# A graph layer on one core: one chain of sums per message, node rows loaded by SyncE, self-loop products placed between products

## The reference, cut to what matters

```
h     = relu(layernorm(x))
W_rel = einsum('rb,bdf->rdf', w_comp, weight)          # 32 types from 8 bases
agg   = segment_sum(h[src] * norm, etype * n_nodes + dst)
node  = einsum('rnd,rdf->nf', agg, W_rel) + h_bias + h @ loop_weight
out   = x + relu(node)
```

## Time and profile before

| | |
|---|---|
| median of three executions | 1019.91 us |
| the profiled execution, own time | 1018.97 us |
| its span | 1017.2 us |
| granted TensorE clock | 0.995 |
| TensorE matmul busy | 992.6 us, 98% |
| VectorE busy | 955.0 us, 94% |
| ScalarE busy | 885.2 us, 87% |
| GpSimd busy | 724.0 us, 71% |
| DMA | 154.47 MB, 152 GB/s |

### The profile page before, as it was taken

How to read it: one execution, slowest core, us unless ns; L and a number is a source line. 1 busy time by engine, 2 the same in 40 slices (tenths; PEclk the granted TensorE clock), 3 DMA queues, 4 the chain that set the end, 5 groups by cost and what they waited for, 6 DMA issues and landing times.

```text
span 1017.2 us, 23777 instructions
## 1 busy us (share of the span) xinstructions
PE 992.6 (98%) x4902; PEld 576.0 (57%) x4902; DVE 955.0 (94%) x4366; ACT 885.2 (87%) x3242; POOL 724.0 (71%) x1282
## 2 busy tenths in 40 slices
PE   5999999999999999999999999999999999999996
PEld 2355555565656555555555555656555555555564
DVE  6999999999999999999999999999999999999994
ACT  6898988889898989898988889898989898988873
POOL 7887777777777777777777776777777776767730
PEclk9999999999999999999999999999999999999998
DMA  4556556556556565565565565655655655655544
GB/s 115 147 138 163 154 151 172 140 153 162 153 148 166 146 163 153 152 166 157 141 171 152 142 172 140 160 159 150 166 150 146 169 148 157 164 149 153 141 126 116
DMA packets 178224, 154.47 MB, mean 152 GB/s; under 512 B 17781, under 2 KB 151213, under 8 KB 178077
## 3 DMA queue, kind: packets, MB, share of 16 engines
q1 hardware_dynamic: 157261, 101.40, 35.8%
q0 software_dynamic: 20384, 51.32, 19.9%
q10 hardware_dynamic: 432, 0.22, 0.1%
HBM read 101.31 MB, written 51.56 MB: 150 GB/s over the span
## 4 chain that ended last, share of the span: by engine, by line
PE 92%; DVE 3%; POOL 2%; issue 2%; DMA 0%; ACT 0%; DVEq 0%; POOLq 0%
PE y_ps L772 33%; PE y_ps L776 31%; PE win_ps L790 10%; PE win_ps L787 8%; PE hT_ps L836 4%; PE hT_ps L782 4%; POOL xg L560 2%; PE mix_ps L828 1%; DVE sum_a L977 1%; DVE sum_b L977 1%; DVE msg L1010 0%; POOL u L505 0%; DMA src_all<-src 0%; DVE nstats L1062 0%; DVE res L1097 0%
## 5 line engine op out<-in xcount | busy, mean ns | idle before, releaser
L560 POOL DMA_INDIRECT xg<-x,idx x392 | 382.0, 974 | 73.3 <-issue 33.7
L772 PE MATMUL y_ps<-w_all,hT 128*128 128x512 f32 x784 | 411.8, 607 | 2.9 <-DVE sum_a L977 2.8
L776 PE MATMUL y_ps<-w_all,hT 128*128 128x512 f32 x784 | 400.3, 592 | 0.0
L505 POOL TENSOR_TENSOR u<-z 128x128 f32<-128x128 f32 x392 | 180.7, 461 | 182.3 <-ACT z L608 178.5
L608 ACT ACTIVATE z<-y_ps,mix 128x128 f32<-128x128 f32 x784 | 245.2, 367 | 44.3 <-PE y_ps L776 44.3
L977 DVE SCALAR_TENSOR_TENSOR sum_b<-y_ps,mix,sum_b 128x128 f32<-128x128 f32 x784 | 265.7, 339 | 0.0
L776 PEld LDWEIGHTS y_ps<-w_all,hT 128*128 128x128 f32 x784 | 149.0, 190 | 187.6 <-issue 160.8
L772 PEld LDWEIGHTS y_ps<-w_all,hT 128*128 128x128 f32 x784 | 132.3, 189 | 119.1 <-DVE sum_a L977 63.8
L604 ACT ACTIVATE z<-y_ps,mix 128x128 f32<-128x128 f32 x392 | 141.2, 360 | 63.0 <-PE y_ps L772 62.8
L642 ACT ACTIVATE hw<-xw,shift,nrstd 128x128 f32<-128x128 f32 x391 | 192.2, 493 | 0.4 <-DVE shift L1079 0.4
L977 DVE SCALAR_TENSOR_TENSOR sum_b<-y_ps,mix,z 128x128 f32<-128x128 f32 x392 | 131.4, 335 | 35.6 <-ACT z L604 35.2
(11 more groups left out here) (102 smaller groups left out, 1159.1 us busy)
## 6 DMA issues: line engine op xcount, KB each, us to landing
seg<-msgs SPq DMA_DIRECT2D x391, 104.8 KB
msgs<-msg SPq DMA_DIRECT2D x98, 258.0 KB, 2.7
xw<-x POOLq DMA_DIRECT2D x97, 256.0 KB
out<-res SPq DMA_DIRECT2D x97, 256.0 KB, 3.1
xg<-x,idx POOLq DMA_INDIRECT x392, 3.2
type_bc<-type_rows SPq DMA_DIRECT2D x52, 112.0 KB
w_all<-weight SPq DMA_DIRECT2D x1, 512.0 KB, 4.2
type_bc<-type_rows SPq DMA_DIRECT2D x4, 80.0 KB
```

The source lines that it names most:

```text
L505: nc.gpsimd.tensor_tensor(u[:, r, :], z[:, r, 0, :], z[:, r, 1, :], ALU.add).then_inc(s_u, 1)
L560: nc.gpsimd.indirect_dma_start(xg[:, q, j, :], None, x, bass.IndirectOffsetOnAxis(ap=idx[:, q, j:j + 1], axis=0)).then_inc(s_gather[q * G ...
L772: nc.tensor.matmul(y_ps[2 * t % 5][:, :, :], hT[:, q, j, :], w_all[:, B // 2:B, :], start=True, stop=True).then_inc(s_y_high, 1)
L776: nc.tensor.matmul(y_ps[(2 * t + 1) % 5][:, :, :], hT[:, q, j, :], w_all[:, 0:B // 2, :], start=True, stop=True).then_inc(s_y, 1)
```

## The change

- **The sums.** The low product comes first. ScalarE scales bases 0, 1 and 2, all of the low product. GpSimd adds the first two into `u` and then, behind a wait for that, the third (`add_three`). VectorE has one chain per tile, `part`: bases 3, 4, 5, 6 on top of `u`, and base 7 goes straight into the message. `idx`, `sum_a` and `sum_b` are gone.
- **Waits of TensorE.** The low product of a tile waits for the message of the tile three back, the high product for base 3 of the tile two back.
- **VectorE's order.** In a tile slot: base 6 of the tile before, node statistics, that tile's message, base 3 of this tile, edge statistics, base 4, aggregation, base 5.
- **The node rows** are loaded by SyncE: two groups after the eighth gather, then one group at the head of each of SyncE's steps.
- **Gathers** read their index column from `src_all`.
- **Self-loop products** of the four windows stand one by one behind the four products of tiles 0 and 1; the window transposes and the edge sums follow them.

```diff
-            return y_ps[(2 * t + (0 if high else 1)) % 5][:, base % (B // 2), :]
+            return y_ps[(2 * t + (1 if high else 0)) % 5][:, base % (B // 2), :]
...
+            sp.wait_ge(s_gather[2 * G - 1], 16)
+            for k in range(X_AT):
+                load_x(k)
+
             for g in range(NGW + OUT_AT):
+                if g + X_AT < NGW:
+                    load_x(g + X_AT)
...
-            def add_pair(t, r):
-                pool.wait_ge(s_z, t + 1)
+            def add_three(t, r):
+                pool.wait_ge(s_z_pair, t + 1)
+                if t >= RING:
+                    pool.wait_ge(s_sum, (B // 2) * (t - RING) + 1)
                 nc.gpsimd.tensor_tensor(u[:, r, :], z[:, r, 0, :], z[:, r, 1, :], ALU.add).then_inc(s_u, 1)
+                pool.wait_ge(s_u, t + 1)
+                pool.wait_ge(s_z_third, t + 1)
+                nc.gpsimd.tensor_tensor(u[:, r, :], u[:, r, :], z[:, r, 2, :], ALU.add).then_inc(s_v, 1)
...
-                    nc.gpsimd.tensor_copy(idx[:, q, :], src_all[:, bass.ds(g * G, G)]).then_inc(s_idx, 1)
-                    pool.wait_ge(s_idx, g + 1)
...
+                act.wait_ge(s_y_low, t + 1)
+                nc.scalar.activation(z[:, r, 0, :], product(t, 0), ACT.Copy, scale=mix[:, q, j, 0:1])
+                nc.scalar.activation(z[:, r, 1, :], product(t, 1), ACT.Copy, scale=mix[:, q, j, 1:2]).then_inc(s_z_pair, 1)
+                nc.scalar.activation(z[:, r, 2, :], product(t, 2), ACT.Copy, scale=mix[:, q, j, 2:3]).then_inc(s_z_third, 1)
...
+            def product_low(g, q, j):
                 t = g * G + j
                 if t >= 3:
-                    pe.wait_ge(s_a, 2 * (t - 2))
+                    pe.wait_ge(s_msg, t - 2)
+                nc.tensor.matmul(y_ps[2 * t % 5][:, :, :], hT[:, q, j, :], w_all[:, 0:B // 2, :],
+                                 start=True, stop=True).then_inc(s_y_low, 1)
+
+            def product_high(g, q, j):
+                t = g * G + j
                 if t >= 2:
-                    pe.wait_ge(s_b, 3 * (t - 1))
+                    pe.wait_ge(s_sum, (B // 2) * (t - 2) + 1)
...
+                        product_low(g - 1, (q - 1) % RING, j)
+                    if k is not None:
+                        window_self(k, 2 * j)
+                    if 1 <= g <= NG:
+                        product_high(g - 1, (q - 1) % RING, j)
+                    if k is not None:
+                        window_self(k, 2 * j + 1)
...
+            def partial(g, q, j, base):
+                t, r = g * G + j, (q * G + j) % RING
+                before = (B // 2) * t + base - 3
+                if base == 3:
+                    dve.wait_ge(s_v, t + 1)
+                    if t >= RING:
+                        dve.wait_ge(s_msg, t - RING + 1)
                     first = u[:, r, :]
                 else:
+                    if base == 4:
+                        dve.wait_ge(s_y, t + 1)
+                    dve.wait_ge(s_sum, before)
+                    first = part[:, r, :]
+                add(part[:, r, :], t, mix[:, q, j, :], base, first).then_inc(s_sum, 1)
...
+                if past:
+                    partial(b[0], b[2], bj, 6)
+                nodes(j)
+                if past:
+                    message(*b, bj)
                 if now:
+                    partial(p[0], p[2], j, 3)
```

More of the change, by code:

```diff
@@ L600, in scale_bases @@
                     act.wait_ge(s_mix, g + 1)
[L601 to L609, removed]
+                if t >= RING:
+                    act.wait_ge(s_v, t - RING + 1)
+                act.wait_ge(s_y_low, t + 1)
+                nc.scalar.activation(z[:, r, 0, :], product(t, 0), ACT.Copy, scale=mix[:, q, j, 0:1])
+                nc.scalar.activation(z[:, r, 1, :], product(t, 1), ACT.Copy, scale=mix[:, q, j, 1:2]).then_inc(s_z_pair, 1)
+                nc.scalar.activation(z[:, r, 2, :], product(t, 2), ACT.Copy, scale=mix[:, q, j, 2:3]).then_inc(s_z_third, 1)
             def group_means(g, n, q):
@@ L783, in window_transposes, with self_loop, edge_sums @@
                 mm.then_inc(n_hT, 1)
-            def sums(v, q, windows):
-                for j in range(windows):
-                    nc.tensor.matmul(win_ps[:, j, :], hwT[:, v, j, :], w_loop[:, :], start=j == 0, stop=False)
+            def self_loop(v, j):
+                nc.tensor.matmul(win_ps[:, j, :], hwT[:, v, j, :], w_loop[:, :], start=j == 0, stop=False)
+            def edge_sums(v, q, windows):
                 for j in range(windows):
@@ L864, in _ @@
                     hold(pe, passed["pe"])
-                    sums(0, 0, G).then_inc(f_y, 1)
+                    for j in range(G):
+                        self_loop(0, j)
+                    edge_sums(0, 0, G).then_inc(f_y, 1)
         @block.vector
@@ L1005, in message @@
             def message(g, n, q, j):
[L1006 removed]
+                t, r = g * G + j, (q * G + j) % RING
                 if j == 0 and not is_before(g, RING):
                     dve.wait_ge(s_stored[q], n * 16)
[L1009 to L1012 removed]
+                dve.wait_ge(s_sum, (B // 2) * (t + 1))
@@ L1015, in tile_slot @@
+                add(msg[:, q, j, 0:F], t, mix[:, q, j, :], B - 1, part[:, r, :]).then_inc(s_msg, 1)
+            def tile_slot(g, n, q, j, more, nodes):
                 now = not is_before(g, 1) and not beyond(g, NG + 1)
@@ L1036, in tile_slot @@
                 if now:
-                    sum_high(p[0], p[2], j, 7)
+                    partial(p[0], p[2], j, 4)
                 if more:
                     dve.wait_ge(s_bn, g * (2 * DV) + (2 * DV + 2 * j + 1))
-                if past:
-                    message(*b, bj)
-                if more:
                     nc.vector.bn_aggr(mv[:, aq, j, :], stats[:, aq, j, :]).then_inc(s_bn, 1)
+                if now:
+                    partial(p[0], p[2], j, 5)
             def one_hot(g, q):
@@ L1113, in stats_of @@
                         window_stats(k, j)
-                tile_slot(g, n, q, 0, more)
-                stats_of(0)
-                tile_slot(g, n, q, 1, more)
-                stats_of(1)
+                tile_slot(g, n, q, 0, more, stats_of)
+                tile_slot(g, n, q, 1, more, stats_of)
                 if here:
```

116 lines of the change are left out of this document (39 added, 77 removed).

## The result

| | before | after |
|---|---|---|
| median | 1019.83 us (4 runs, 1018.57 to 1020.28) | 1029.72 us (4 runs, 1028.68 to 1030.68) |
| profiled execution, own time | 1018.97 | 1028.68 |
| span | 1017.18 | 1026.81 |
| mixing product of step 1 | 22.07 | 22.38 |
| of step 6 | 68.01 | 73.29 |

The ratio is 1.0099, 95% interval [1.0087, 1.0112]: slower, by 9.9 us. The time lies in the predicted range, 7.3 above the predicted 1022.4. From start to the mixing product of step 6 the kernel after loses 5.28 us (forecast 1.7), in the next 91 steps 4.26 (forecast 0), behind them 0.09 (forecast 0.8): 9.63, the difference of the spans.

A forecast was written before the change was run, and what follows sets the result against it. TensorE, full in 913.5 of 1017.2 us, was taken as the bound. 1018.97 + 1.7 (warm-up) + 0 x 91 (steady steps) + 0.8 (tail) = 1021.5, as a median 1022.4 us; range 1015.5 to 1032.

The forecast's parts named there:

- rival 1: Steady state: GpSimd's second addition waits longer for the first and stalls TensorE; 1029 us at 0.20, 1040 at 0.27; chance 0.25.
- Steady step: One TensorE step of four message tiles, from step 6 on: stays 10.04 us.
- the 0.10 at the edge sums: TensorE's delay before the first edge product, given to the change of form and kept whatever stands ahead; 0.10 us a step.
- Rival 2: TensorE's change to edge products is free behind a transpose, so 0.10 leaves each of 92 steps; 1013 us; chance 0.10.
- The chain that I had laid along the old durations: New order from ScalarE's scalings through GpSimd's additions to VectorE's tile 1 message, ending 11.85 us behind the mixing product.
- 0 x 91: Steady part: no change in any of the 91 steps between the mixing products of step 6 and the last.
- The slack of 0.25: Steady step: tile 1's message is ready 0.25 us before TensorE's first product of the next step's tile 0 needs it.
- some 9.0: GpSimd's full round with the second additions and without node-row load and index copy, segment work included; under the 10.04 us step.
- Warm-up: Before step 6 GpSimd's longer round sets the pace; mixing product of step 6 at 69.7 instead of 68.01, +1.7 us.
- Rival 3: Warm-up: VectorE's relief and a GpSimd lead recover half of some 5.5 us of stalls; 1018 to 1020 us; chance 0.10.
- Tail: Behind the last mixing product: message store +0.4 and transposes between the last self-loop products and edge sums +0.4; +0.8 us.
- The row of 0.36: VectorE: a dependent addition starts 0.36 us after its predecessor, an independent one 0.26; six of twenty give 0.6 back.

The follow-up runs named there:

- e4: The kernel before with every part of the change except the sums (two chains, one GpSimd addition per tile kept); 1017.44 us, ratio 0.9981.
- e2: The kernel after with GpSimd's wait for the last gather of the group three before put back; 1027.86 us, ratio 1.0097.
- e3: The kernel after with group 1's reciprocal ahead of tile 1's slot on VectorE and its gain ahead of tile 1's additions on GpSimd; 1027.21 us, ratio 1.0083.
- e5: e4 plus a second GpSimd addition per tile that waits for the first and writes a buffer nobody reads; 1021.75 us, ratio 1.0027.
- e9: e3 with VectorE's one-hot matrix for the segments moved behind the mixing coefficients; 1027.36 us, ratio 1.0075.
- e1: The kernel after with the node rows loaded on GpSimd's queue again, one load per step; 1081.66 us, ratio 1.0613.
- e8: The kernel before with only node rows loaded by SyncE and gathers reading the full index array; 1017.31 us, ratio 0.9986.
- e6: e3 with node rows of one group in eight loaded by GpSimd's queue, the others by SyncE; 1031.51 us, ratio 1.0124.
- e10: e8 with VectorE's one-hot matrix for the segments moved behind the mixing coefficients; 1016.65 us, ratio 0.9973.

## Why the prediction was right, and where its sizes were not

The sign held. That the time lies in the range is luck: the likeliest case's own range was 1019.5 to 1025, and 1029.7 is outside it. It is inside the wide range only because that was drawn for rival 1, whose 1029 came from a wait inside GpSimd's pair of additions that did not occur. The forecast was +2.5 us, the measured change is +9.9.

**Steady step: right.** 10.03, the 0.10 at the edge sums kept, whatever stands ahead of them. Rival 2 (the change of form free behind a transpose) is out. The second addition starts 0.53 to 0.55 behind the first (387 of the 392 times) and not 0.73, so rival 1's mechanism is out as well, though its place, the first product of tile 0 waiting for the message, is where the long steps lose their time. The chain that I had laid along the old durations was close: it had the message of tile 1 end 11.85 - 10.04 = 1.81 us behind the mixing product, and in the step shown above it ends 508.27 + 0.34 - 506.86 = 1.75 behind it.
```profile
508.27 0.34 DVE L992 SCALAR_TENSOR_TENSOR msg<-y_ps,mix,part 128x128 f32<-128x128 f32 x1
```

**"0 x 91": wrong by 4.3.** The step that failed is that I took every steady step to be like the one I laid out. Three gathers come 2 us late. e4 shows that holds exist without the chain and cost nothing there; after, e2 and e3 that with the chain each costs 1.3 to 1.6. e5 points to the order of the chain and not the full GpSimd alone, but with shorter holds. The slack of 0.25 worked out for the message of tile 1 gives (1.97 - 0.15) - 0.25 = 1.57 for the first hold, and its two steps are 1.47 + 0.10 too long. For the second the same sum gives 1.73 against 1.26, and e9 shows that more slack at that one place only moves the wait: the fit of the first is no proof. A first sign of it stood in the trace of before, the 12 late loads with their 6.7 us, and I did not look at it: 0.55 us under 1.8 us of idle time cost nothing. With the second addition the idle time went.

**GpSimd's round: undersized.** Forecast "some 9.0", measured 9.66. The missing 0.66 is the gain instruction: in the warm-up round that I started from it took 0.21 with no idle time ahead of it, in the round shown it takes 0.62 with 0.28 ahead (over the whole trace 0.60 with 0.35, before 0.40 with 0.05). Why it takes longer there no run shows. So the room was 0.37 and not 1.0 us a step, and e1 shows how much hung on that: moving the node rows to SyncE, which I had priced at nothing but GpSimd's relief, is what keeps this kernel from 1080.

**Warm-up: mis-sized, 1.7 against 5.3.** I worked it out from GpSimd's round alone, "with hardly a wait". To set the parts apart I use the kernels whose step 1 lies between 22.0 and 22.6, and the stretch up to step 5, in which e9's moved instruction does not occur yet. From the mixing product of step 1 to that of step 5 it takes 35.1 before, 33.2 in e4, 36.1 in e5, 38.5 in e9 and 39.9 after. So the dropped load and copies give -1.9, a second addition's time +2.9, the order of the chain +2.4, the gain behind the additions +1.5 (1.3 if step 1 is not taken off): 4.8 together. Each is the difference of two single profiles, and the idle addition of e5 is 0.40 long where the real one takes 0.46, so up to 0.8 of the 2.4 (16 tiles) belongs to the addition's time. The first two have the sign and, with +1.0 together, roughly the size that I gave them; the two that I had not are waits of the engines for each other: in a filling pipeline a chain that passes GpSimd before VectorE starts each tile later, and TensorE waits for the message three tiles back. Rival 3 is out.

**Tail: +0.8 forecast, not settled by the 0.09.** From the last mixing product to the end of the last result it is 31.0 us (before 31.8), and the last store and the end take 4.7 instead of 3.9. But the two tails ran at different clocks. Stretch, length, busy time of PE, PEld, VectorE, ScalarE and GpSimd, granted clock, DMA share, GB/s; first before, then after:
```profile
1007.00:1017.18 10.18, 4.83 (x34) 3.84 (x34) 1.81 (x3) 0.00 (x0) 0.20 (x1) 0.50 0.29 86
...
1007.80:1011.20 3.40, 3.26 (x16) 2.96 (x18) 1.23 (x7) 1.27 (x4) 0.00 (x0) 0.50 0.44 108
1011.20:1024.90 13.70, 7.65 (x89) 6.31 (x85) 4.13 (x8) 3.87 (x9) 0.40 (x2) 1.00 0.54 144
```
Before, the last 10.2 us had half the clock; after, 3.4 of them and the last 1.9. Two profiles kept the full clock up to their last result: e8, with the tail's old order, takes 29.6 us from the last mixing product to there, e6, with the new one, 30.2. By these two the new order costs 0.6, near the forecast, but no experiment changed the tail alone.

**VectorE's pitches.** The row of 0.36 for a dependent sum against 0.26 carries over and is a little larger: two sums of one chain right behind each other start 0.39 apart in the kernel after (274 pairs from 100 us on, all alike). One such pair, 0.35 each:
```profile
268.38 0.74 DVE L992 SCALAR_TENSOR_TENSOR part<-y_ps,mix,part 128x128 f32<-128x128 f32 x2
```
VectorE's busy share fell to 91%, and that was worth nothing, as said.

Open: what the hold is. The Trainium skill (page "DMA: Bandwidth & Descriptors", section "SWDGE vs HWDGE vs iDMA") says that GpSimd itself writes the descriptors of its DMAs into rings that the DMA engines drain. A fixed count between holds fits with such a ring coming round, but no run here shows a ring, and the counts (102 gathers; 28 gathers with 7 loads; 160 with 5 for two holds) fit no one size of a gather and a load: the first two would make a load 10.6 gathers, the first and the third 8.8. Nor does it say why the same hold is 1.2 us long in one kernel and 2 in another.

## What to carry to other kernels

An engine with much waiting time on the page is a buffer as much as it is room: work moved to it costs nothing in the mean step and takes away what hid its rare late starts. Work out its full round from a stretch in which it is catching up, gaps and all, and read the small lines of the table of waits for events that come seldom. In a warm-up, count the engines that wait for each other, tile by tile; the longest round of one engine is only a lower bound. And time the parts of a change apart: here the parts without the chain of sums gained 0.14% to 0.19%, and the chain lost 1.2%. Where two single profiles are compared over a few tens of microseconds, look at the granted clock of both first.

## What the runs showed of the hardware

- A DMA that GpSimd issues starts late at fixed counts of what its queue has carried: gathers 114, 216 and 318 in after, e2 to e5 and e8 to e10. With the chain (after, e2, e3, e9) 1.9 to 2.5 us of idle time stand ahead of it, with two chains (e4, e5, e8, e10) 1.2 to 1.4, against 0.15 ahead of other gathers. Gather 114 comes at 264 us in one kernel and at 272 in another: it goes by count and not by time.
- With a load of 256 KB in each round beside four gathers (before, e1) the hold is 0.55 us, every seventh round.
- TensorE's clock rises at different moments of the start. In e8 its first weight loads are 0.85 us apart up to 19.43 us, and 0.43 from 20.2 us on; e3 turns at 20.1, the kernel after at 18.1. TensorE had been at work since 14.2, 14.0 and 13.9 in them. Step 1 is then 1.1 us later. The two pitches are a factor of two apart, the two levels of 1.2 and 2.4 GHz. With two chains the 1.1 us are still there at step 6 (e8 against e4); with the chain and the gain first only 0.2 are left at step 5 (e3 against e9).
- The clock also falls for stretches: in the warm-up of e1 to 0.50 for 3.4 us from 35.6 (TensorE had been busy 3.4 of the 5.6 us ahead), and in the tail to 0.50 for the last 10.2 us of the kernel before (TensorE had been busy 21.3 of the 25.5 us ahead), for 3.4 us from 1007.8 in the kernel after (14.3 of 16.7), not at all before the last result in e6 and e8.
- A GpSimd addition that needs the one before it starts 0.54 us behind it, and a gather behind an addition 0.15 after its end.
